# A two-layer graph network on one core: finding the unit borders by a two-level search instead of histograms, and adding layer two's own rows by an identity product

## What is computed

```python
h = jnp.maximum(_layernorm(x, axis=-1), 0.0)
x = x + _L0_gnn_ref(h, relation_embedding, W1, b1, w2, edge_index, edge_type_200)
h = jnp.maximum(_layernorm(x, axis=-1), 0.0)
x = x + _L1_gnn_ref(h, src, dst)
```

```python
agg = jax.ops.segment_sum(feats[src], dst, num_segments=n_nodes)
out = jnp.where((deg > 0)[:, None], agg, feats)
```

## Time and profile before

| | us |
|---|---|
| median of 3 runs | 1927.12 |
| lowest and highest | 1917.56 and 1928.97 |
| the profiled execution | 1914.29 |
| its span, first to last instruction | 1910.0 |

### The profile page before, as it was taken

The page is one execution under the profiler, slowest core; times in us unless marked ns, Lnnn a source line. Parts: engine busy times, 40 slices in busy tenths (PEclk is TensorE's granted clock), DMA queues, the critical chain, the costliest instruction groups (busy, mean ns, idle before and its releaser), DMA issues.

```text
span 1910.0 us, 37271 instructions
## 1 busy us (share of the span) xinstructions
PE 1499.3 (78%) x11712; PEld 1398.7 (73%) x11712; DVE 1659.8 (87%) x5669; ACT 1372.7 (72%) x3555; POOL 1294.4 (68%) x1090
## 2 busy tenths in 40 slices
PE   1148999999999999999999943666766676667666
PEld 1148999999999999999999842555655565556555
DVE  5456899999999999999999777999898999899997
ACT  0048888888888888888888624667776776667676
POOL 1467887777777777777773017777777777777772
PEclk9569999999999999999999985566565555565666
DMA  0175566666666556666665581666665666666534
GB/s 13 42 181 137 139 177 173 175 161 163 173 173 178 161 162 174 170 180 163 161 171 145 139 224 37 179 172 180 173 175 158 180 171 176 173 170 183 136 101 110
DMA packets 465579, 296.71 MB, mean 155 GB/s; under 512 B 32756, under 2 KB 434734, under 8 KB 465382
## 3 DMA queue, kind: packets, MB, share of 16 engines
q1 hardware_dynamic: 430534, 242.10, 46.2%
q0 software_dynamic: 34848, 52.23, 11.1%
HBM read 207.54 MB, written 103.74 MB: 163 GB/s over the span
## 4 chain that ended last, share of the span: by engine, by line
PE 49%; DVE 13%; ACT 9%; issue 8%; DMA 8%; POOL 7%; SPq 1%; POOLq 0%; DVEq 0%; ACTq 0%
POOL xe L994 7%; DMA xe<-x_d,idx_t 7%; PE c_p L1340 7%; PE c_p L1341 6%; PE t_p L1328 6%; ACT cs L1266 5%; PE c_p L1345 5%; PE c_p L1343 5%; PE y_p L1362 4%; PE t_p L1327 3%; ACT cs L1269 3%; PE t_p L1330 3%; PE t_p L1329 3%; PE y_p L1364 3%; PE y_p L1365 3%
## 5 line engine op out<-in xcount | busy, mean ns | idle before, releaser
L994 POOL DMA_INDIRECT xe<-in_x,idx_t x522 | 682.4, 1307 | 256.4 <-issue 150.2
L994 POOL DMA_INDIRECT xe<-x_d,idx_t x522 | 579.9, 1111 | 268.5 <-issue 131.0
L1028 DVE BATCH_NORM_STATS2 st<-xn 128x6 f32<-128x128 f32 x1566 | 349.3, 276 | 119.9 <-DMA xe<-x_d,idx_t 86.4
L1266 ACT ACTIVATE cs<-xn,nbias,rstd 128x128 f32<-128x128 f32 x783 | 326.3, 480 | 43.9 <-DVE nbias L1072 43.9
L1266 ACT ACTIVATE an<-xn,nbias,rstd 128x128 f32<-128x128 f32 x783 | 326.8, 482 | 13.0 <-DVE nbias L1072 13.0
L1030 DVE BATCH_NORM_STATS2 st<-xe 128x6 f32<-128x128 f32 x1044 | 243.0, 273 | 0.0
L1292 ACT ACTIVATE lr<-y_p 128x390 f32<-128x390 f32 x261 | 129.4, 496 | 137.5 <-PE y_p L1365 133.2
L1269 ACT ACTIVATE ae<-xe,nbias,rstd 128x128 f32<-128x128 f32 x522 | 226.1, 481 | 0.0
L1269 ACT ACTIVATE cs<-xe,nbias,rstd 128x128 f32<-128x128 f32 x522 | 225.4, 479 | 0.0
L1340 PE MATMUL c_p<-w1a,th 128*128 128x129 f32 x1044 | 216.0, 289 | 0.0
L1341 PE MATMUL c_p<-w1b,th 128*128 128x129 f32 x1044 | 202.2, 275 | 0.0
(11 more groups left out here) (183 smaller groups left out, 3750.8 us busy)
## 6 DMA issues: line engine op xcount, KB each, us to landing
xn<-in_x SPq DMA_DIRECT2D x130, 384.0 KB, 6.6
x_d<-xn SPq DMA_DIRECT2D x130, 384.0 KB, 7.5
xn<-x_d SPq DMA_DIRECT2D x130, 384.0 KB, 4.5
out<-xn SPq DMA_DIRECT2D x130, 384.0 KB, 3.7
plr<-place_d SPq DMA_DIRECT2D x65, 256.0 KB, 3.5
tyr<-types_d SPq DMA_DIRECT2D x65, 256.0 KB, 5.5
xe<-in_x,idx_t POOLq DMA_INDIRECT x522, 3.2
xe<-x_d,idx_t POOLq DMA_INDIRECT x522, 2.7
```

What stands on the lines that cost most here:

```text
L994: nc.gpsimd.indirect_dma_start(out=xe_of(L, u)[:, e, :], out_offset=None, in_=a, in_offset=bass.IndirectOffsetOnAxis(ap=idx_t[:, j:j + 1], ...
L1028: v.bn_stats(st[:, j % 2, UN * at + i, :], xs_of(L, u)[:, i, :])
L1266: a(own[:, i, :], xs_of(L, u)[:, i, :], ACT.Relu, bias=nbias[:, j % 2, c:c + 1], scale=rstd[:, j % 2, c:c + 1])
```

## The change

**Finding the borders.** The histogram goes. DVE puts dst, src and type side by side, as fp32, into one table of three numbers an edge (tab), which SP stores to DRAM. The edges form 256 rows of 196. PE turns the rows' first dst values to all units' partitions; a comparison and a count give each unit the row in which it begins (L725 to L730 of the new kernel), POOL gathers that row of dst (three gathers, L671), and a second comparison and count give the first edge (L745 to L749). POOL gathers the first window, three numbers an edge, in three gathers (L679); DVE counts how many of its edges belong to the tile's range, which gives the start of the second window (L762 to L767), gathered in three more.

**What stands where.** SP loads src and type with dst at the start, and issues the loads of the first five blocks of x inside the set-up. The set-up no longer waits for its stores of places and types; SP waits for them in the main part. The copy to plc_t, the three-way split of the relations and the scan masks now open DVE's main part, and the masks' store stands behind the first tables in SP's. POOL's memset of xe stands between the row gathers and the window gathers.

**Layer two.** own2 goes. PE opens the sums of a unit with a product of the identity with the own rows (128x384, fp32), and the four selection products add to it. ACT no longer waits for L2.own.

The core of the diff:

```diff
-                for c in range(4):
-                    wait(dve, k_tr, c)
-                    r32 = row32[:, :].unsqueeze(1).to_broadcast([P, CH, 32])
-                    v.tensor_tensor(oh_h, hi_f[:, c * CH:(c + 1) * CH].unsqueeze(2).to_broadcast([P, CH, 32]), r32, ALU.is_equal)
...
+                dve.wait_ge(k_dst, 16)
+                steps.then(v.tensor_copy(tab[:, :, 0], dsti))
+                v.tensor_copy(firsts, tab[:, ::HALF, 0].unsqueeze(2).to_broadcast([P, 2, TU])).then_inc(k_first, 1)
...
+                dve.wait_ge(k_firstT, 1)
+                steps.then(v.tensor_tensor(less1, first_p.unsqueeze(1).to_broadcast([TU, TC, 2 * P]),
+                                           base[:, :, 0:1].to_broadcast([TU, TC, 2 * P]), ALU.is_lt))
+                steps.then(v.tensor_reduce(cnt1, less1, AX, ALU.add))
...
+                v.tensor_copy(row_at, r2).then_inc(k_row, 1)
+                dve.wait_ge(k_edge, 32)
+                v.tensor_copy(tab[:, :, 1], srci).then_inc(k_tab, 1)
+                v.tensor_copy(tab[:, :, 2], typi).then_inc(k_tab, 1)
...
+                for k in range(TC):
+                    dve.wait_ge(k_rowl[k], 16)
+                    steps.then(v.tensor_tensor(less2[:, k, :], rows_i[:, k, :], base_i[:, k:k + 1].to_broadcast([TU, HALF]), ALU.is_lt))
...
+                pool.wait_ge(k_row, 1)
+                for k in range(TC):
+                    g.indirect_dma_start(out=rows_i[:, k, :], out_offset=None, in_=dst_e,
...
                 g.memset(xe[:, :, :, :], 0.0)
+                pool.wait_ge(k_tabs, 16)
+                for e in range(UE):
+                    for k in range(TC):
+                        pool.wait_ge(k_win[e], k + 1)
+                        g.indirect_dma_start(out=gwin[:, k, e, :, :].rearrange("p c t -> p (c t)"), out_offset=None, in_=tab_d,
...
+                for q in range(XPRE):
+                    for rows_, g0, g1, np_ in parts_of(x, q):
+                        sp.dma_start(xn[0:np_, q, g0:g1, :], rows_).then_inc(x_in.of(q), 16)
...
-                for q in range(5):
-                    load_x(L1, x, q)
+                sp.wait_ge(k_out, 32)
                 for q in range(2):
                     load_tables(q)
+                sp.wait_ge(k_scan, UE + 1)
...
+                for j in range(2):
+                    v.tensor_copy(plc_t[:, j * TC * TU:(j + 1) * TC * TU], y_p[:, j, 0:TC * TU])
+                for c, n in ((0, P), (1, RB)):
+                    rel_part(c, n)
+                scan_masks()
...
-                    if s % 2 == 0:
-                        own2(s // 2)
...
-                        wait(act, L2.own, (u - 8) // 2 + 1)
...
+                    if L is L2:
+                        mm(y[:, 0:UN * D], ident[:, :], own2_[:, u % 8, :, :].rearrange("p i d -> p (i d)"), start=True, stop=False,
+                           skip_group_check=True)
```

More of the change, by code:

```diff
@@ new lines, in gnn_two_layers @@
+        dsti, srci, typi = (part(EC, start=A0 + EC * i).bitcast(i32) for i in range(3))
+        tab = part(3 * EC).rearrange("p (c t) -> p c t", t=3)
+        wrong = part(EC)
+        less1 = part(TC * 2 * P)[0:TU].rearrange("p (k f) -> p k f", f=2 * P)
+        mt = scratch[0:TU, A0:A0 + TC * 4 * SLOTS].rearrange("p (k a s) -> p k a s", a=4, s=SLOTS)
+        firsts = part(2 * TU).rearrange("p (h u) -> p h u", u=TU)
+        nextp, bad, badf = part(1).bitcast(i32), part(2), part(1)[0:1, :]
+        B0 = taken[0]
@@ L661, in _ @@
[L661 to L664 removed]
+                steps.then(g.memset(ident[:, :], 0.0))
                 g.affine_select(out=ident[:, :], in_=ident[:, :], compare_op=ALU.not_equal, fill=1.0, base=0,
                                 pattern=[[-1, P]], channel_multiplier=1)
[L667 to L668 removed]
@@ new lines, in _ @@
+                pe.wait_ge(k_relTs, 1)
+                nc.tensor.matmul(t_p[:, 1, 0:P], relT[:, 0:P], w1s[:, 2, :], start=True, stop=True)
+                nc.tensor.matmul(t_p[0:RB, 1, P:2 * P], relT[:, P:P + RB], w1s[:, 2, :], start=True, stop=True).then_inc(k_relw, 1)
+                for e in range(UE):
+                    for table, to, made, turned_ in ((pq, y_p, k_plc, k_plcT), (idf, c_p, k_idx, k_idxT)):
+                        pe.wait_ge(made, e + 1)
+                        for k in range(TC):
+                            j = UE * k + e
+                            last = nc.tensor.transpose(to[:, j // TC, j % TC * TU:j % TC * TU + TU], half(table, e)[:, k, :],
+                                                       ident[0:TU, 0:TU])
+                        last.then_inc(turned_, 1)
@@ L824, in _ @@
-                for j in range(2):
-                    last = v.tensor_copy(idx_t[:, j * TC * TU:(j + 1) * TC * TU], c_p[:, j, 0:TC * TU])
-                last.then_inc(k_ready, 1)
+                for k in range(TC):
+                    dve.wait_ge(k_winl[1][k], 16)
+                steps.then(v.tensor_tensor(pl[:, :, 1, :], gwin[:, :, 1, :, 0], base[:, :, 1:2].to_broadcast([TU, TC, P + 1]), ALU.subtract))
+                steps.then(v.tensor_scalar(fo[:, :, 1, :], pl[:, :, 1, :], float(SLOTS), None, ALU.is_ge))
@@ L1396, in gnn_two_layers, with _ @@
         with nc.Else(), ExitStack() as ctx3:
+            with nc.Block() as block:
+                @block.sync
+                def _(sp):
+                    for q in range(XPRE):
+                        sp.wait_ge(x_in.of(q), x_in.count(q))
+                    sp.wait_ge(k_out, 32)
             general_path(nc, ctx3, sem, general_buffers, x, src_e, dst_e, typ_e, out)
```

341 lines of the change are left out of this document (140 added, 201 removed).

## The result

The new kernel takes 1813.19 us (median of 4 runs, 1812.32 to 1815.92), the old one beside it 1927.9 us (4 runs, 1917.56 to 1928.97): ratio 0.9427, interval 0.9405 to 0.9449. Forecast were 1821 us and a range of 1800 to 1866. The profiled execution took 1812.44 us with a span of 1807.6; the old span was 1910.0, so 102.4 us are gone where 106 were forecast. On the median's scale it is 114.7 us, because the old kernel's runs lay up to 14.7 us above its profiled one and the new kernel's lie within 3.5 us of theirs. That holds for this chip; on two others the gain was far smaller, and the experiments are mostly about that.

What follows compares the result with a forecast made beforehand. POOL's start was taken to bound layer one's start, PE its steady part, POOL's gather rate layer two. Set-up 56 plus layer two 50 made 106 us: 1808 us profiled, 1821 us on the median's scale, range 1800 to 1866.

Steps and rivals of the forecast that it cites:

- (a): Set-up, loading node indices into SBUF: the first load alone was expected to be in at 4.7 us.
- (b): Set-up, first search level on DVE and PE (cast, copy, transposes, comparison, reduction, casts): 4.2 us, row addresses at 8.9.
- (c): Set-up on POOL: three row gathers end at 13.7 us, then the memset of xe until 17.2; landing and counts hidden.
- (d): Set-up, three window gathers from 17.3 to 21.9 us, landing in 4.7 us beside the x loads: in at 26.6.
- (e): Set-up, six small DVE steps for the last of the first window gathers: 1.3 us, done at 27.9.
- (f): Set-up, the second windows' last gather: 1.4 + 4 us, in at 33.3.
- (g): Set-up, places, ids, tables, two copies of ids and the flag: 4.6 us, done at 37.9.
- (h): From DVE's end of set-up to POOL's first layer-one gather: 4.20 us before, 3.7 without SP's store wait, reaching 41.6.
- What moved behind the start: Relation splitting and scan masks on DVE ahead of layer one's first statistics: stalled steps cost 3 us.
- Layer two's gathers: On POOL, without DVE's own-rows additions, a gather falls from 1.416 to 1.32 us: 50 us gained, ends 0 and 59.
- PE and its clock: Layer two's identity product on PE costs no time; PE is given its clock, mean 0.62 to 0.85, busy above 75%.
- C: Rival: PE never has the full clock in layer two, short waits breaking its work up: 1968 us, slower; chance 0.03.

Runs made afterwards that it cites:

- e6: New kernel with SP's ten x loads held back until the second windows are asked for: 1810.41 us, ratio 0.9442 to the kernel before, chip 2.
- e8: New kernel with row comparison before the weights' wait, memset behind the first window gathers, two x blocks loaded late in the set-up: 1991.42 us, ratio 0.9846, chip 4.
- e3: New kernel plus one unused 768-column DVE addition per two units in layer two, both inputs in SBUF: 1990.2 us, ratio 0.9848, chip 3; repeated on chip 4: 0.9864.
- e4: New kernel plus the same unused DVE addition, but with its second input in PSUM: 2011.41 us, ratio 0.9953, chip 3; repeated on chip 4: 0.994.
- e9: New kernel with layer two's identity product over only 128 of the 384 columns, other own rows left out: 1810.45 us, one run, chip 2.
- e2: Kernel before, old set-up kept, with the identity product in place of own2 and its wait: 2041.1 us, ratio 1.0107, chip 3.
- e7: New kernel with the row comparison before the wait for the weights and the memset of xe ahead of the row gathers: 1809.59 us, ratio 0.9435, chip 2.

## Why the prediction was right, and where its terms were off

**The sum: right, the last step by luck.** The spans give 102.4 us where 106 were forecast: 51.65 us up to layer two (56), 48.1 in it (50), 2.6 behind it (0). The profiled run came out at 1812.44 us, 4.4 above the 1808 forecast for it. The median is 7.8 us below the 1821, since the 12.8 us that I added for the runs' spread were 0.75. No row of one trace could give this term; had it stayed, 1825 us would have been measured.

**What bounds what: right.** POOL is the clock of layer two before and after, with DVE the one that waits, and the start of layer one takes the whole of the set-up's gain: 52.65 us at the first gather, 51.65 us still there at layer two's first.

**The set-up: right in kind, 6.4 us too hopeful** (41.6 forecast, 48.05 measured, inside the 37 to 49; the gain is at the lower end of the 52 to 65 forecast). The new kernel's timeline of the set-up:

```profile
3.23 0.43 DVE L719 CAST xn<-xn 128x392 f32<-128x392 int32 x1 [3.23 <-DMA xn<-in_dst]
...
7.69 1.55 POOL L671 DMA_INDIRECT xn<-in_dst,xn  x1 [5.57 <-DVE xn L730]
...
8.73 2.08 SPq L644 DMA_DIRECT2D xn<-in_w  x1
...
11.33 15.91 SPq L648 DMA_DIRECT2D xn<-in_x  x10
12.40 3.53 POOL L674 MEMSET xe<- 128x4096 f32 x1
17.39 0.37 DVE L741 COPY xn<-t_p 128x200 f32<-128x200 f32 x1 [9.41 <-PE t_p L696]
...
19.87 1.28 POOL L679 DMA_INDIRECT xn<-tab_d,xn  x1 [3.95 <-DVE xn L749]
...
27.29 0.32 DVE L762 TENSOR_TENSOR xn<-xn 87x128 f32<-87x128 f32 x1 [3.42 <-DMA xn<-tab_d,xn]
...
33.20 0.32 DVE L762 TENSOR_TENSOR xn<-xn 87x128 f32<-87x128 f32 x1 [1.33 <-DMA xn<-tab_d,xn]
...
34.95 1.44 POOL L679 DMA_INDIRECT xn<-tab_d,xn  x1 [1.52 <-DVE xn L767]
...
40.37 0.66 DVE L790 TENSOR_TENSOR xn<-xn 87x387 f32<-87x387 f32 x1 [0.51 <-DMA xn<-tab_d,xn]
```

Step by step, length forecast and measured: (a) 4.7 and 3.2 us; (b) 4.2 and 4.5; (c) from the row gather to the first window gather 8.4 and 12.2; (d) until the last window is in 9.3 and 13.3; (e) 1.3 and 1.75; (f) 5.4 and 5.4; (g) 4.6 and 5.0; (h) 3.7 and 2.7. Two steps failed.

In (c) I let POOL's memset decide and called the counts hidden. POOL was free at 15.93 and waited 3.95 us for DVE, and DVE stood 9.41 us in front of the copy of the transposed relations, for PE, which waits for the last small load. SP's issue of the one before it took 2.08 us, and the last one itself, asked for at 10.85 with the x loads behind it from 11.33, lets PE start at 16.68. That the weights stand on this path I had not seen. In e6, which keeps the order, the first window gather is at 18.97; in e8, with the comparison ahead of that wait and the memset out of the way, at 15.18, 4.7 us sooner than in the new kernel. e8 doesn't say how much of it is the one and how much the other.

In (d) I took 4.7 us for a landing beside the x loads, from a bracket of 3.5 to 5.5; from its start to DVE's use of it the three took 7.4, 9.0 and 9.9 us. e6, without the loads at that point, shows 5.0 for the first. The prediction named "more than 6 us after their issue" as the sign of an error there, and so it was. One slip of reading cost nothing: of the eight one-hot comparisons before, three wait for PE and not four.

**What moved behind the start: right, smaller.** The 44th gather is 58.13 us behind the first: 1.2 us more than before, where I had 3.

**Layer two's gathers: right.** 1.323 us a gather against 1.32; 48.1 us gained against 50. The mechanism, gathers lengthened by an addition with two SBUF inputs, is shown by e3 and e4, twice. By this the first sentence that I quoted from the Trainium skill's "SBUF — State Buffer", section "Who interferes with whom" (two SBUF inputs contend with a GpSimd instruction that reads SBUF), is borne out with 1126 against 1001 ns. The inference beside it, that tensor_tensor leaves descriptor writing alone, is not borne out for these gathers, which take their row numbers from SBUF.

**PE and its clock: right in sign, too low in size.** I forecast a mean clock of 0.62 to 0.85 and a busy share above 75%; it was 0.91 and 71% (460.60 of 650). What failed is the thought that PE is given only the clock that it needs to keep pace: by the prediction's estimate 0.62 would have done, and e9 has 0.79 with fewer columns than now. What decides the rest is open; for the time it made no difference. C is refuted here: PE waits for DVE's selections dozens of times in layer two, for up to 6 us, and has the full clock most of the time. The section of "TensorE: Matmul & The Clock Gate" in the Trainium skill that the prediction names beside C tells of waits of several us for data in each turn of a loop; PE's waits before, in 1200 to 1740, were 191 with a mean of 0.9 us, 13 of them over 2 us, so that it says little about most of them.

**The tail:** nothing forecast, 2.6 us gained.

**What the prediction did not have at all** is the chip. Its layer-two half rests on POOL issuing without a pause, which is true on the first two chips (no pause over 0.35 us); on two others it is not, and the whole change gives 1.2% in place of 5.7%. That isn't a wrong sum but a condition that no row of one trace could show.

## What to carry to other kernels

Find the engine whose instructions follow each other with nothing but the issue gap, and ask what lengthens a single one of them: a DVE addition off the path cost POOL 0.37 us on average (48.1 us over 131 additions), and moving it to an engine with room, even as more work there, won 6.5% of the stage (48.1 of 737.6 us) where POOL issues without a pause. In a set-up of dependent steps, look at what each queue does at that moment: bulk loads issued beside a small gather cost it 2 to 5 us wherever I moved them, and a POOL memset of 3.5 us cost the DVE cast or copy beside it 2.2 to 3.6 us. And time a change on more than one chip before its size is believed: a gain that rests on one engine never pausing is gone on a chip where the others pause.

## What the hardware showed that I had not expected

- The kernel before takes 1918 to 1928 us on chips 1 and 2 and 2022 to 2027 us on two others, with standstills of several us in layer two (the longest 18.6 us on ACT and 38.0 on PE in e2's trace); the new set-up is of the same length on all (48 us). The clock doesn't explain it: the kernel before has a mean clock of 0.78 to 0.83 on each of them. PE's pauses without a visible cause do go with it, 49 to 123 us of 540 against 0.2 at the most. Their cause is open.
- On those chips shorter gathers gave no time back (e2 took 19.5 us more than the kernel before).
- A memset on POOL stops a DVE copy or cast of fp32 or int32 to fp32 in SBUF until it ends: 0.43 us became 2.65 (e7), 0.60 became 4.17 (e8). The Trainium skill's "SBUF — State Buffer", section "Who interferes with whom", has this as a lock on the ports shared by DVE and GpSimd that is held for a whole instruction, and the traces agree: the cast ends within 0.3 us of the memset, the two copies within 0.2. The section also says that whoever issues first has the ports; in e8 the first copy starts at 19.11, 0.55 us before the memset at 19.66, and is held up all the same, so the start times don't show that part.
- An indirect gather of one row for each of 87 partitions can be used 5.0 us after its start with no x load beside it (e6), and after 7.4 to 9.9 us beside ten loads of 384 KB (new kernel).
- PE's granted clock in layer two rose with the work put into it (0.79, 0.91, 0.98) although every version had waits in it.
